# Attention block on eight cores: x1 of seven groups transposed by DMA through DRAM, both halves of U1 behind the scores, and transposes given ahead of sums

## The reference

```python
q = x @ Wq;  k = x @ Wk;  v = x @ Wv                    # 1024 x 1024 each
scores = q @ k.T, masked above the diagonal             # causal
attn = softmax(scores / 32)
x1 = layernorm(x + (attn @ v) @ Wo)
P = x1 @ U1                                             # 1024 x 256
H = gelu(P @ V1 + b1)                                   # 256 x 4096
Q = H @ U2                                              # 4096 x 256
out = layernorm(x1 + Q @ V2 + b2)                       # 256 x 1024
```

## Time and profile before

| | us |
|---|---|
| median of 3 runs | 1611.42 (1611.37 to 1696.34) |
| profiled execution, device time | 1610.35 |
| profiled execution, span of the slowest core | 1608.7 |
| spans of the eight cores | 1606.0 to 1608.7 |

### The profile page before, as it was taken

One profiled execution on the slowest core, in us unless ns is written; L12 is line 12 of the kernel. 1 busy time (PEld: TensorE's weight loads), 2 busy tenths in 40 slices (PEclk: granted clock), 3 DMA queues, 4 the chain that ended last, 5 costly groups with the idle time before them and its releaser, 6 DMA issues.

```text
span 1608.7 us, 26838 instructions; the slowest of 8 cores (1606.0 to 1608.7 us)
## 1 busy us (share of the span) xinstructions
PE 1553.5 (97%) x8656; PEld 790.2 (49%) x8816; DVE 706.1 (44%) x1442; ACT 598.3 (37%) x1241; POOL 91.5 (6%) x137
## 2 busy tenths in 40 slices
PE   6999999999999999999999999999999999999996
PEld 2555455454445454454544544544554544455455
DVE  2437266445544364432645323536330733632154
ACT  3633613631463044620446400445510244641025
POOL 0021010001000100000000010000000000000000
PEclk9999999999999999999999999999999999999998
DMA  9899998665575623939245675345658344204601
GB/s 285 273 250 193 153 107 257 134 123 180 179 136 110 205 79 118 117 114 307 75 145 109 88 226 198 105 157 119 80 169 266 118 167 146 92 32 153 209 1 54
DMA packets 72049, 242.51 MB, mean 151 GB/s; under 512 B 4960, under 2 KB 10224, under 8 KB 61296
## 3 DMA queue, kind: packets, MB, share of 16 engines
q1 hardware_dynamic: 60320, 190.86, 36.3%
q0 software_dynamic: 11600, 49.93, 21.2%
HBM read 252.40 MB, written 52.43 MB: 189 GB/s over the span
## 4 chain that ended last, share of the span: by engine, by line
PE 94%; ACT 2%; issue 1%; DMA 1%; DVE 1%; DVEq 0%; SPq 0%; POOLq 0%; ACTq 0%
PE ps L698 28%; PE ps L666 27%; PE ps L753 7%; PE ps L855 7%; PE ps L649 7%; PE ps L743 7%; PE ps L682 3%; PE ps L639 2%; PE ps L807 2%; PE ps L770 2%; PE ps L627 2%; PE ps L781 1%; DMA wf<-wkt 1%; ACT p_sb L898 1%; ACT p_sb L975 0%
## 5 line engine op out<-in xcount | busy, mean ns | idle before, releaser
L698 PE MATMUL ps<-p_sb,x_ring 128*128 128x512 bf16 (+3 forms) x2248 | 463.1, 362 | 11.7 <-ACT p_sb L975 8.7
L666 PE MATMUL ps<-x_ring,zt 128*128 128x512 bf16 (+3 forms) x2169 | 443.5, 363 | 1.7
L698 PEld LDWEIGHTS ps<-p_sb,x_ring 128*128 128x128 bf16 x2304 | 218.4, 98 | 234.7 <-issue 10.3
L666 PEld LDWEIGHTS ps<-x_ring,zt 128*128 128x128 bf16 x2208 | 210.1, 98 | 226.9
L1024 DVE TENSOR_REDUCE nm<-ps 128x1 f32<-128x512 f32 (+2 forms) x288 | 185.7, 647 | 257.0 <-PE ps L666 250.2
L898 ACT ACTIVATE p_sb<-ps,nm 128x512 bf16<-128x512 f32 (+2 forms) x288 | 187.1, 652 | 237.4 <-DVE nm L1024 237.1
L916 ACT ACTIVATE zt<-ps,b_sb 128x512 bf16<-128x512 f32 (+1 forms) x288 | 174.6, 645 | 33.7 <-PE ps L743 31.8
L753 PE MATMUL ps<-zt,wf 128*128 128x512 bf16 (+1 forms) x569 | 150.4, 355 | 5.2 <-ACT zt L916 4.8
L743 PE MATMUL ps<-p_sb,wf 128*128 128x512 bf16 (+1 forms) x563 | 149.4, 355 | 1.3 <-DVE p_sb L1042 0.5
L1170 DVE CAST ot<-ps 128x512 bf16<-128x512 f32 x32 | 22.1, 692 | 274.7 <-PE ps L698 274.7
L888 ACT ACTIVATE ot<-ps 128x512 bf16<-128x512 f32 x32 | 19.1, 598 | 294.1 <-PE ps L698 294.1
(11 more groups left out here) (83 smaller groups left out, 963.4 us busy)
## 6 DMA issues: line engine op xcount, KB each, us to landing
x_ring<-xtb SPq DMA_DIRECT2D x67, 1024.0 KB, 5.4
x_ring<-xnb SPq DMA_DIRECT2D x48, 1024.0 KB, 6.4
xnb<-xn POOLq DMA_DIRECT2D x8, 2048.0 KB, 41.8
x<-xo SPq DMA_DIRECT2D x24, 512.0 KB, 9.9
xtb<-xt POOLq DMA_DIRECT2D x12, 1024.0 KB, 25.9
out<-x POOLq DMA_DIRECT2D x24, 512.0 KB, 7.8
x_ring<-xnb SPq DMA_DIRECT2D x16, 768.0 KB, 6.2
wf<-wvt SPq DMA_DIRECT2D x8, 512.0 KB, 18.4
```

The lines of the kernel that those rows point to most:

```text
L666: mm = t.matmul(ps[b][:, 0:w], zt[:, ec * 512 + j * 128:ec * 512 + (j + 1) * 128], xs[:, off + ec * 512:off + ec * 512 + w], start=(ec == ...
L698: mm = t.matmul(ps[b][:, q0:512], ring[:, off + k * step:off + k * step + 128], P[:, p0 + q0:p0 + 512], start=(c == 0 and k == 0), stop=(c ...
```

## The change

Three edits.

1. For groups 0 to 6 x1 is no longer transposed by TensorE. SP stores `x16` to a DRAM tensor `x1s` (1 MB, one of two places in turn), waits for it, and reads it back into `ot` by eight transfers of 512 x 128 with `transpose=True`. For group 0 this stands behind `store_turned(3)`, for the others behind the load for step t = 4 of the next group's S. ACT waits for the store (`d_x16`) ahead of the exponentials of step 2 of the next group, because these overwrite `x16`. PE waits for the eight transfers (`d_xt`) ahead of P1. Group 7 is transposed by PE as before.
2. Both tiles of P1 stand behind all of S. DVE rescales four tiles ahead of the two copies of P1 and the rest of the early ones behind them.
3. In the loop over the chunks the transposes of chunk c + 2 are given ahead of the sums of chunk c, but for c = 0.

```diff
@@ def psum_numbers():
...
             scores(g, range(last))
-            for j in range(3):
-                put(ring, ring_out, ("s", g, last, j), "exp")
-            put(ring, ring_out, ("p1", g - 1, 0), "p1")
-            put(ring, ring_out, ("s", g, last, 3), "exp")
-            put(ring, ring_out, ("p1", g - 1, 1), "p1")
+            scores(g, range(last, last + 1))
+            projected(g - 1, ())
...
         if g + 1 < NG:
-            turned_x1(g, range(4))
-        if g + 1 < NG:
             for f in range(5, 8):
...
@@ SyncE
+            def turn_x1(g):
+
+                s.wait_ge(s_x16, 4 * (g + 1))
+                s.dma_start(out=x1s.ap()[g % 2].rearrange("(j p) e -> p j e", p=128),
+                            in_=x16.rearrange("p (j e) -> p j e", j=4)).then_inc(d_x16, 16)
+                s.wait_ge(d_x16, 16 * (g + 1))
+                for k in range(8):
+                    s.dma_start(out=ot[:, k * 512:(k + 1) * 512],
+                                in_=x1s.ap()[g % 2, :, k * 128:(k + 1) * 128],
+                                transpose=True).then_inc(d_xt, 16)
+
+            turn_x1(0)
             s.wait_ge(s_full, RING[("s", 1, 3, 3)] + 1)
...
                     load_scores(g, t)
+                    if t == 4:
+                        turn_x1(g - 1)
...
@@ TensorE
-                for j in range(q0 // 128, (q0 + n) // 128):
-                    for h in range(2):
-                        emptied(("xt", g, j, h))
+                if g < NG - 1:
+                    t.wait_ge(d_xt, 128 * (g + 1))
+                else:
+                    for j in range(q0 // 128, (q0 + n) // 128):
+                        for h in range(2):
+                            emptied(("xt", g, j, h))
...
-                    for ti in range(nt - 1):
+                    for ti in range(nt):
                         score_tiles(g, ti)
-                    score_tiles(g, nt - 1, range(3))
-                    ffn_in(g - 1, 0)
-                    score_tiles(g, nt - 1, range(3, 4))
-                    ffn_in(g - 1, 1)
+                    for rc in range(2):
+                        ffn_in(g - 1, rc)
...
                     for j in range(4):
                         emptied(("t", g, c, j))
+                    ahead = later_turns(g, c + 2) if c + 2 < nt else []
+                    if c > 0:
+                        for _, j in ahead:
+                            turn_tile(g, c + 2, j)
                     if c < nt - 2:
                         for e in range(2):
                             values_chunk(g, e, c)
-                    if c + 2 < nt:
-                        for _, j in later_turns(g, c + 2):
+                    if c == 0:
+                        for _, j in ahead:
                             turn_tile(g, c + 2, j)
...
                 if more:
-                    turn_x1(g, range(4))
                     for f in range(5, 8):
                         z_tile(g + 1, f)
...
@@ ScalarE
                     for ti in range(2 * g + 2):
+                        if ti == 2:
+                            sc.wait_ge(d_x16, 16 * g)
                         exps(g, ti)
...
-                for j in range(4):
-                    for h in range(1 if more else 2):
+                for j in range(0 if more else 4):
+                    for h in range(2):
                         tile_full(sc, ("xt", g, j, h))
...
@@ VectorE
                     for c, j in early[:2]:
                         rescale(g, c, j)
-                    ffn_in(g - 1, 0)
                     row_max(g, nt - 1, 3)
-                    for c, j in early[2:]:
+                    for c, j in early[2:4]:
                         rescale(g, c, j)
-                    ffn_in(g - 1, 1)
+                    for rc in range(2):
+                        ffn_in(g - 1, rc)
+                    for c, j in early[4:]:
+                        rescale(g, c, j)
...
-                for j in range(4 if g < NG - 1 else 0):
-                    tile_full(v, ("xt", g, j, 1))
-                    b = psb[RING[("xt", g, j, 1)] % RB]
-                    v.tensor_copy(x1_turned(j, 1), b[:, 0:512].rearrange("p (n k) -> p n k", k=128)
-                                  ).then_inc(out_of["xt_dve"], 1)
...
```

More of the change, by code:

```diff
@@ L115, in turned_x1 @@
             for h in range(2):
-                put(ring, ring_out, ("xt", g, j, h), "xt_act" if h == 0 or g == NG - 1 else "xt_dve")
+                put(ring, ring_out, ("xt", g, j, h), "xt_act")
     def ffn_out(g, js=range(4)):
@@ L248, in build_program @@
     xnb = nc.dram_tensor("xnb", [8, 8, 128, 1024], BF16, kind="Internal")
+    x1s = nc.dram_tensor("x1s", [2, 512, 1024], BF16, kind="Internal")
     mscr = nc.dram_tensor("mscr", [128, 8192], BF16, kind="Internal")
@@ L313, in build_program @@
             "m_act", "m_dve", "w_act", "w_dve", "xp_act", "xp_dve", "z", "exp", "turn_act", "turn_dve", "ot_act",
-            "ot_dve", "x1", "xt_act", "xt_dve", "p1", "q2", "gelu", "r2")}
+            "ot_dve", "x1", "xt_act", "p1", "q2", "gelu", "r2")}
         d_u1, d_v1, d_u2, d_v2 = S("d_u1"), S("d_v1"), S("d_u2"), S("d_v2")
@@ L321, in build_program @@
         d_out, d_last = S("d_out"), S("d_last")
+        d_x16, d_xt = S("d_x16"), S("d_xt")
         s_const = S("const")
```

## The result

The changed kernel takes 1640.8 us (median of 4, 1635.1 to 1645.2) against 1611.4 (median of 3): a ratio of 1.018, interval 1.0147 to 1.0213. It is slower, though the interval leaves open whether by 2%, and it lies outside the range of 1589 to 1624. All times here are of fast runs; the chip has a slower state, in which a fourth run of the kernel before took 1696.3 us. The profiled execution took 1635.1 us with a span of 1633.5 on core 3.

The account below looks back on a forecast made before the run. The prediction took TensorE to bound the kernel, with 94% of the chain of waits. Its terms, -14.7 - 7.5 + 1.0 + 8 = -13.2 us, gave 1598 us against 1611.4, with a range of 1589 to 1624.

Parts of the forecast that it names:

- Transposes off PE: In groups 0 to 6, removing TensorE's transposes of x1 saves 2.78 + 6 x 1.98 = 14.7 us.
- Transposes ahead of sums: At the loop's end in groups 1 to 7, eight sums fill PE's idle gap of 0.94 to 1.16 us, saving 7.5 us.
- The 0.3 us margin at chunk 3: DVE's adds of V2 end 0.3 us before the third transpose of chunk 3 needs their bank; costed at nothing.
- P1 behind S: At the end of S, the hidden layer starts 0.1 to 0.2 us later in six groups: +1.0 us, bounds 0 and +2.5.
- ACT's wait for the store: In group 0 the store of x16 lands by 161.8; PE needs the bank at 164.8, so the wait is covered by 3 us.
- Groups from 2 on have room: Transfers cost nothing from group 2 on: group 1 has 44 us of room, each later group 14 us more.
- The transfers of group 0 take 14 us, at most 44, so P1 waits 8 us: At the end of S, the eight transfers land at 176, needed at 168.3: +8 us, bounds 0 and 38.
- The slow rival: Slow transposing transfers make P1 wait over 20 us, cancelling the gains; 1638 us at 44.4 us per megabyte; chance 0.14.

Follow-up runs that it names:

- e1: The changed kernel with group 0's x1 transposed by TensorE, groups 1 to 6 still by transfers: 1592.8 us, ratio 0.989 to the kernel before.
- e4: The kernel before with only the third edit, transposes of chunk c + 2 ahead of the sums of chunk c: 1602.9 us, ratio 0.9954.
- e5: The kernel before with only the second edit, both tiles of P1 behind S and DVE's order with it: ratio 1.0009.
- e6: e1 with the second edit taken back, so P1 stands around the last block of S again: 1591.3 us, ratio 0.988 to the kernel before.
- e2: The changed kernel with GpSimd's casts of chunks 4 and 5 issued only when group 0's transfers have landed: 1603.6 us, ratio 0.996 to the kernel before.
- e13: The changed kernel with U2's four loads issued behind group 0's transfers: 1622 us; the eight transfers took 10.1 to 10.8 us to issue.
- e3: The changed kernel with group 0 on TensorE and scratch casts or copies issued with the store in groups 2 to 4: the eight took 10 to 12 us.
- e8: The changed kernel with group 0 on TensorE, scratch transfers issued once the store landed: two casts in group 2 made the eight take 25 to 28 us.
- e11: The changed kernel with the casts of chunks 4 and 5 issued only when group 0's store has landed: the eight took 21.6 to 42.1 us to issue.

## Why the prediction was wrong

- **Transposes off PE, -14.7.** Right as far as tested: e1 has the six groups, 11.9 us of it, and its sum comes within 0.7 us. Group 0's 2.8 us stand in no run by themselves.
- **Transposes ahead of sums, -7.5.** Right: e4 gives 0.46%, 7.4 us of 1610.9. The 0.3 us margin at chunk 3 held.
- **P1 behind S, +1.0.** Right in place, somewhat low in size: 1.4 us by e5, 1.5 to 2 by e6 against e1, and at most 1.8 by the waits in the trace.
- **ACT's wait for the store is covered.** Right. The store landed 6 us earlier than forecast.
- **Groups from 2 on have room.** Right, and the quiet price of the eight, 11 us to issue and 4 to land, is even the 14 us that I took.
- **The transfers of group 0 take 14 us, at most 44, so P1 waits 8 us.** This term failed. With their landing they took 29 us on the best core and 55 on the slowest, there over the upper bound. I priced them by the plain store of chunk 3 in the same stretch, 10.2 us, and raised it only a little for pieces of 256 bytes. That row was not of the company it was taken for. The prediction put all 97.2% of GpSimd's queue down to the two casts; by the packet records of core 0, 46.5 of them are U2's pieces and 35.6 the casts, and no cast packet moved before 154.8, when that store had landed (151.6). So it shows what a plain store costs beside U2, and the eight were to run beside the casts. What the runs showed in place of the 14 us: the quiet price is 15 us, and the company makes the rest. Without casts beside them (e2) the eight are quiet; without U2's loads ahead of them (e13) the casts are through before the eight start; with both the eight take 27 to 52 us to issue. The store of x16 was no guide either: it took 17 us there against 5 quiet, a factor of 3, and the eight up to 51.6 against 10 to 11.6, a factor of 5. That pieces of 256 bytes suffer more from the same company is not shown by this: beside two casts alone the store went from 5 us to between 21 and 24 (e3), the eight from 10 to between 25 and 28 (e8).
- **The end of the term was read for one core.** The wait was 16.7 to 44.1 us by core. With casts and small pieces in flight the time varies from core to core, and the slowest of eight is the time of the kernel. For core 0 alone, from which the rows were read, the wait was 23.5 us and the span went from 1608.7 to 1611.1; the forecast would have missed by less, but still the wrong way.
- **The slow rival** had the wait and the point where it decides, 28 us, and its 1638 us is near 1640.8. That nearness is partly luck: 10 of its 48 us are a wait of the next group that no core shows, and it lacks the clock's 2.7 us and the spread of the cores. Its case for itself, small pieces in a stretch with no free DMA time, was the argument to follow; I gave it 0.14. The estimate from the Trainium skill's VectorE: DVE Perf Modes, The three transpose paths, 42 us for the 32 blocks, was near for group 0 but for another reason: in quiet groups the same eight are done in 15 us.

What stays open is what in the engines or the memory holds a 256-byte piece for that long, and how much each of U2 and the casts has in the 27 to 52 us: with the casts issued late (e11) the eight take 22 to 42, though U2's packets end within 12 us of their start on seven cores.

## What to carry to other kernels

Work taken off the bounding engine and put on DMA is only free where the stretch has free DMA time; read the DMA share of every place where the new transfers will run, not the mean, and leave the one place that has none as it was. List every transfer that is in flight there, and ask of each when it moves and not when it is issued (here 20 us lay between), and take the price for the slowest of the cores. Moving one of the neighbours away can move the loss and not end it: e2 put it on a load of x, e13 on the store. An order that lets the bounding engine wait for a copy behind other work of its own gave 7.4 us here.

## What the runs showed of the hardware

A quiet transposing transfer of 512 x 128 bf16 from DRAM costs SP about 1.3 us to issue and lands in some 4 us; eight move 1 MB in 15 us. The packets of SP's queue (q1) in two windows of core 3 of the changed kernel, 180 to 200 us and 436 to 460 us (packets, MB, share of 16 engines):

```profile
q1 hardware_dynamic: 825, 0.20, 138.1%
...
q1 hardware_dynamic: 5130, 4.00, 63.9%
```

In the first a packet, nearly all of 256 bytes, is held for 1.381 x 16 x 20 / 825 = 0.54 us on the mean; in the second, four in five of them as small, for 0.639 x 16 x 24 / 5130 = 0.048 us. The mean hides how it is spread. In the trace's own records of these 825 packets 632 took at most 0.1 us, and 144 took 1.5 to 4.9 us and make 93% of the time. Over all eight transfers of group 0, 4096 pieces, those held for 1.5 us or more and the issue time rise together from core to core:

| core | 4 | 0 | 2 | 5 | 7 | 1 | 6 | 3 |
|---|---|---|---|---|---|---|---|---|
| pieces of 256 bytes held for 1.5 us or more | 20 | 68 | 98 | 103 | 118 | 120 | 167 | 194 |
| the eight, us to issue | 27.5 | 33.4 | 38.4 | 40.9 | 40.5 | 42.8 | 48.2 | 51.6 |

In group 2 of core 3 none was held so long. So a few pieces stand for a long time, and the others pass as fast as in a quiet group. I had not expected that from two casts and the loads of U2, nor that plain copies from ScalarE's queue, GpSimd's and SP's own hold the eight nearly alike.
